# First pass of a two-layer attention kernel: half of the pair tiles after the image tiles, beside the statistics

## Chip, cores and metric

One core of a Trainium2 chip runs the kernel. The metric is the device time of one execution in microseconds, the median of three runs. TensorE (PE, with its weight load PEld), VectorE (DVE), ScalarE (ACT), GpSimd (POOL) and SyncE (SP, which here issues every DMA) each run their own instruction stream and wait on semaphores.

## What is computed

Two attention layers over x of shape (1, 128, 256, 256), each with a group norm before it and a residual after it. Cut to what matters here:

```python
# layer 0: h = group_norm(x); then
mu, var = mean and variance of h over all of (C, H, W)
x0   = (h - mu) * rsqrt(var + EPS) * ln_w + ln_b              # ln_w, ln_b: (128, 256, 256)
bias = einsum('hc,bcij->bhij', wb, x0)                        # 4 heads, from the image itself
...                                                           # q, k, v, g; softmax(q k + bias) v, gated, projected
x = x + layer0(h)
# layer 1: h = group_norm(x); then
bias = einsum('nijz,zh->nhij', pair_repr, bias_proj)[:, None] # 8 heads, from pair_repr (1, 256, 256, 128)
sim  = softmax(q k * scale) + bias                            # bias after the softmax
x = x + (sim v * gate) @ out_proj
```

The group norm's groups are the 8 last-axis columns, 32 groups; each needs the mean and variance over the whole image, so layer 0 can't begin before all of x has been read once.

## The kernel before

`prepare_weights` loads and splits the weights and starts the loads of the first two image tiles. `first_pass` then reads the image, the layer norm's weights and bias and the pair representation once, in 32 tiles of 8 rows. One image tile is three DMAs of 1 MB (x, ln_w, ln_b, line 209), one pair tile a DMA of 1 MB (line 243). All have two buffers. For each tile:

- DVE takes batch-norm statistics of the 32 groups (line 328), six numbers a group and tile, and POOL then multiplies x by ln_w in place (line 341).
- PE turns the pair tile by 16 transposes of 128x128 in four strips, one PSUM bank each (line 290). ACT copies strips 0 and 2 to SBUF (line 313), DVE strips 1 and 3 (line 303).
- PE projects ln_w, ln_b, the turned pair tile and x * ln_w onto the heads, eight matmul records each (line 277). ACT copies the four results to `fp_evac` (line 317), and SP stores them in eight small DMAs to the HBM scratch tensors `image_bias_parts` (line 256) and `pair_bias` (line 257).

SP's order for a tile: wait until the tile's buffers are free (all projections of it done, its pair tile turned), issue the four loads for the tile after next, then wait for the copy out and issue the eight stores.

When the pass's block is over, `finish_statistics` (first call) begins a new one. SP reads the three parts (six DMAs of 512 KB, line 378) and the pair bias (two of 1 MB, line 380) into SBUF. DVE aggregates 32 chunks of six numbers per group (line 386, 32 instructions of 192 elements); PE averages over the partitions with two small matmuls (lines 452, 454); DVE and ACT work out inverse roots of the group norm and of the layer norm; four DVE products over 128x2048 correct the layer 0 bias (lines 424 to 427). Then `layer0` runs 256 rows, storing its output and its statistics. `finish_statistics` (second call) aggregates those (33 chunks), turns layer 1's bias by 32 transposes beside it (lines 434 and 448), and `layer1` runs 128 rows of heads.

## Time and profile before

| | us |
|---|---|
| median of three runs | 4951.82 (4950.63 to 4952.84) |
| profiled execution | 4953.47 |
| its span | 4951.5 |
| PE busy | 4653.2 (94%) |
| DVE busy | 4023.9 (81%) |
| ACT busy | 3527.3 (71%) |
| POOL busy | 3466.7 (70%) |
| mean granted TensorE clock | 0.97 |

The span runs from the first instruction to the last, and the profiled execution has 2 us more around it. The page gives engine shares over the whole span, and PE's 94% is that of the two layers. The first pass and its statistics are the first 470 us, less than a tenth. There the other views are needed: windows give busy time, clock and DMA by stretch; the timeline gives each instruction's start and length, and in brackets how long its engine had been idle and what released it. A granted clock of 1.00 stands for 2.4 GHz and 0.50 for 1.2 GHz.

### The profile page before, as it was taken

What the parts mean: (1) busy time and instruction counts of PE and PEld (TensorE: products, weight loads), DVE (VectorE), ACT (ScalarE), POOL (GpSimd) and SP (SyncE); (2) the same over time, 40 slices, a digit from 0 to 9 for tenths busy, and PEclk for the clock granted to TensorE, in tenths of its full rate; (3) what the DMA queues carried; (4) which work ended last, traced back from release to release, by engine and by line L of the source; (5) the groups of instructions that cost most, each with busy time, mean ns of one, the idle gap of its engine ahead of it and who ended that gap; (6) DMA issues with size and microseconds to landing.
All of it is one profiled execution on the core that took longest, in us unless ns stands there. A gap on an engine that the chain in (4) does not pass through costs nothing. (4 is left out here: it accounts for less than half of the span.)

```text
span 4951.5 us, 149914 instructions
## 1 busy us (share of the span) xinstructions
PE 4653.2 (94%) x44087; PEld 3924.4 (79%) x44087; DVE 4023.9 (81%) x12779; ACT 3527.3 (71%) x11216; POOL 3466.7 (70%) x5926
## 2 busy tenths in 40 slices
PE   4663999999999999999999969999999999999999
PEld 2332888888888888888888858888888888888887
DVE  4445888888888888888888878888888888888887
ACT  2222888888888888888888846666666666666665
POOL 2332888888888888888888826666666666666665
PEclk8776999999999999999999979999999999999999
DMA  8995111111111111111111101111111111111111
GB/s 331 354 350 176 53 51 59 59 51 59 55 55 59 51 59 59 51 59 56 54 59 51 53 26 53 48 49 49 51 51 51 51 51 51 51 51 51 51 50 39
DMA packets 237329, 382.52 MB, mean 77 GB/s; under 512 B 18756, under 2 KB 156616, under 8 KB 224968
## 3 DMA queue, kind: packets, MB, share of 16 engines
q1 hardware_dynamic: 237256, 381.63, 23.0%
q8 instruction: 35, 0.57, 0.0%
q14 instruction: 38, 0.31, 0.0%
HBM read 309.21 MB, written 72.35 MB: 77 GB/s over the span
## 5 line engine op out<-in xcount | busy, mean ns | idle before, releaser
L1302 POOL TENSOR_SCALAR l_probs<-l_probs,l_inv 128x256 f32<-128x256 f32 x2048 | 944.3, 479 | 737.1 <-DVE l_inv L1207 731.7
L1126 ACT ACTIVATE l_probs<-bank,l_neg_max 128x256 f32<-128x256 f32 x2048 | 949.1, 482 | 486.2 <-DVE l_neg_max L1201 486.2
L545 POOL TENSOR_SCALAR l_probs<-l_probs,l_inv 128x256 f32<-128x256 f32 x2048 | 949.4, 479 | 269.0 <-DVE l_inv L796 269.0
L714 ACT ACTIVATE l_probs<-l_probs,l_neg_max 128x256 f32<-128x256 f32 x2048 | 1020.0, 518 | 1.5 <-DVE l_neg_max L788 1.3
L788 DVE CUSTOM_DVE_ANT_0 l_probs<-bank,bias 128x256 f32<-128x256 f32 x2048 | 779.8, 418 | 219.8 <-PE bank L655 215.6
L1201 DVE TENSOR_REDUCE l_neg_max<-bank 128x2 f32<-128x512 f32 x1024 | 646.7, 683 | 92.6 <-PE bank L1035 92.6
L1214 DVE TENSOR_TENSOR l_probs_t<-bank,bias 128x512 f32<-128x512 f32 x1024 | 674.1, 681 | 37.7 <-PE bank L1045 22.6
L655 PE MATMUL bank<-ident,l_probs 128*128 128x128 f32 x4096 | 629.4, 276 | 1.0 <-POOL l_probs L545 0.6
L1045 PE MATMUL bank<-ident,l_probs 128*128 128x128 f32 x4096 | 532.4, 273 | 3.1 <-DVE l_probs_t L1214 1.7
L668 PE MATMUL bank<-l_probs_t,l_v 128*64 128x256 f32 x4096 | 498.5, 385 | 0.7 <-DVE l_probs_t L810 0.5
L655 PEld LDWEIGHTS bank<-ident,l_probs 128*128 128x128 f32 x4096 | 463.9, 141 | 36.7 <-POOL l_probs L545 1.7
L1045 PEld LDWEIGHTS bank<-ident,l_probs 128*128 128x128 f32 x4096 | 460.6, 141 | 5.7 <-POOL l_probs L1302 3.3
L754 ACT ACTIVATE l_probs_t<-bank 128x512 f32<-128x512 f32 x512 | 309.2, 604 | 211.7 <-PE bank L655 211.7
L1126 ACT ACTIVATION_READ_ACCUMULATOR l_probs<-bank,l_neg_max 128x1 f32 x2048 | 434.8, 212 | 0.0
L714 ACT ACTIVATION_READ_ACCUMULATOR l_probs<-l_probs,l_neg_max 128x1 f32 x2048 | 429.6, 210 | 0.0
L810 DVE COPY l_probs_t<-bank 128x512 f32<-128x512 f32 x512 | 349.6, 683 | 53.6 <-PE bank L655 52.1
L668 PEld LDWEIGHTS bank<-l_probs_t,l_v 128*64 128x64 f32 x4096 | 271.7, 136 | 143.8 <-issue 1.1
L80 PE MATMUL bank<-l_xn_high,wqk_high 128*128 128x256 f32 x1024 | 331.2, 323 | 25.7 <-POOL l_xn_low L572 25.4
L642 PE MATMUL bank<-l_k_high,l_q_high 64*128 64x256 f32 x2048 | 342.0, 331 | 1.6 <-DVE l_k_low L804 1.6
L557 POOL TENSOR_TENSOR l_xf<-l_x,mean 128x256 f32<-128x256 f32 x256 | 301.5, 1178 | 58.7 <-DMA l_ln_b<-in_L_conv_ln_b_dram 58.7
L341 POOL TENSOR_TENSOR fp_x<-fp_x,fp_ln_w 128x2048 f32<-128x2048 f32 x32 | 145.6, 4549 | 268.4 <-DVE chunk_stats L328 268.4
L80 PE MATMUL bank<-l_xn_high,w_qk_high 128*128 128x256 f32 x1024 | 310.4, 303 | 3.5 <-POOL l_xn_low L1291 3.5
(193 smaller groups left out, 14002.8 us busy)
## 6 DMA issues: line engine op xcount, KB each, us to landing
fp_x<-in_x_dram SPq DMA_DIRECT2D x32, 1024.0 KB, 6.9
fp_ln_w<-in_L_conv_ln_w_dram SPq DMA_DIRECT2D x32, 1024.0 KB, 8.9
fp_ln_b<-in_L_conv_ln_b_dram SPq DMA_DIRECT2D x32, 1024.0 KB, 10.2
fp_pair<-in_L_conv_pair_repr_dram SPq DMA_DIRECT2D x32, 1024.0 KB, 12.1
l_x<-in_x_dram SPq DMA_DIRECT2D x128, 256.0 KB, 2.9
l_ln_w<-in_L_conv_ln_w_dram SPq DMA_DIRECT2D x128, 256.0 KB, 3.3
l_ln_b<-in_L_conv_ln_b_dram SPq DMA_DIRECT2D x128, 256.0 KB, 3.5
x<-l_y SPq DMA_DIRECT2D x128, 256.0 KB, 2.0
```

Source lines behind the costliest of these rows:

```text
L80: nc.tensor.matmul(out, lh, rh, start=start, stop=False)
L545: last = nc.gpsimd.tensor_scalar(probs[:, h, c], probs[:, h, c], inv[:, h, c:c + 1], 1.0, ALU.mult, ALU.mult)
L655: last = nc.tensor.transpose(b_t[h % 2][:, kc * W + qc * P:kc * W + (qc + 1) * P], probs[:, h, qc, kc * P:(kc + 1) * P], m.ident[:])
L668: last = nc.tensor.matmul(b_av[D0 * j:D0 * (j + 1), pair * W:(pair + 1) * W], v[:, k % 2, kc, h * D0:(h + 1) * D0], probs_t[:, k % 2, h, k ...
L714: last = nc.scalar.activation(probs[:, h, c], probs[:, h, c], ACT.Exp, bias=neg_max[:, h, c:c + 1], scale=-1.0, accum_out=total[:, h, c:c ...
L788: last = nc.vector.tensor_tensor_reduce(out=probs[:, h, c], in0=b_s[h % 2][:, c * W:(c + 1) * W], in1=m.bias0[:, c, h], scale=-1.0, scalar ...
L810: nc.vector.tensor_copy(probs_t[:, k % 2, h], b_t[h % 2][:].rearrange("p (a c) -> p a c", a=KC)).then_inc(t_ready[h], 1)
L1045: last = nc.tensor.transpose(b_t[TURNS.index(h) % 2][:, kc * W + qc * P:kc * W + (qc + 1) * P], probs[:, h, qc, kc * P:(kc + 1) * P], m.id ...
L1126: last = nc.scalar.activation(probs[:, h, c], b_s[h % 4][:, c * W:(c + 1) * W], ACT.Exp, bias=neg_max[:, h, c:c + 1], accum_out=total[:, h ...
L1201: nc.vector.tensor_reduce(neg_max[:, h], b_s[h % 4][:].rearrange("p (a c) -> p a c", a=KC), AX.X, ALU.max, negate=True).then_inc(max_ready, 1)
L1214: nc.vector.tensor_tensor(probs_t[:, k % 2, h], b_t[TURNS.index(h) % 2][:].rearrange("p (a c) -> p a c", a=KC), m.bias1[:, :, h], ALU.add) ...
L1302: last = nc.gpsimd.tensor_scalar(probs[:, h, c], probs[:, h, c], inv[:, h, c:c + 1], 1.0, ALU.mult, ALU.mult)
```

## The change

In `first_pass`, a pair tile now follows every second image tile, so that pair tiles 0 to 15 are handled beside the 32 image tiles. The pair work is split from the image work: turned strips are copied by ACT alone, the pair projection has its own copy out and its own four stores, the image parts have four stores of their own.

After the image tiles SP waits for the image stores, reads the parts back into SBUF within the same block, and then handles pair tiles 16 to 31 (`late_pairs`): for each, the load of the tile two further on, then the stores of this one. On PE the turns of the next tile stand ahead of the projection of this one, and on ACT likewise the copies. The two averaging matmuls stand in PE's order behind the projections of tiles 18 and 19, ACT's two roots behind tiles 20 and 22.

DVE aggregates the statistics of every four tiles in the pass into pieces (count 1, mean, variance), 32 instructions of 24 elements each; after the pass it aggregates eight pieces a group, and then does the same chain and the same four products as before. The chain's code is now in a class `Statistics` that both places use. The first call of `finish_statistics` is gone. The second one now loads layer 1's bias from HBM itself, before its transposes.

```diff
+class Statistics:
...
+    def vector(self, dve, pieces, with_layer_norm):
+        for g in range(NG):
+            last = nc.vector.bn_aggr(own[:, g, :], pieces(g))
+        last.then_inc(self.own_ready, 1)
+        chain = Chain(dve, self.step)
+        dve.wait_ge(self.own_ready, 1)
+        dve.wait_ge(self.mean_mm, 1)
...
+    def tensor(self, pe, n):
+        nc, m = self.nc, self.m
+        if n == 0:
+            pe.wait_ge(self.own_ready, 1)
+            nc.tensor.matmul(m.psum[0][:, 0:2 * NG], m.averager[:], self.own[:].rearrange("p g s -> p (g s)"), start=True, stop=True).then_inc(self.mean_mm, 1)
+        else:
+            pe.wait_ge(self.dev_ready, 1)
+            nc.tensor.matmul(m.psum[1][:, 0:NG], m.averager[:], self.dev[:], start=True, stop=True).then_inc(self.dev_mm, 1)
...
-    PAIRS = ROWS // 2
-    STORES = 2 * PAIRS
-    X_PART, W_PART, B_PART, PAIR_PART = range(4)
+    STRIPS = ROWS // 2
+    PERIOD = 4
+    X_PART, W_PART, B_PART = range(3)
+    b_part, b_pair, b_turned = m.psum[0:3], m.psum[3], m.psum[4:8]
...
+        def over_tiles(engine, image_tile, pair_tile):
+            def body(t):
+                for k in range(PERIOD):
+                    image_tile(PERIOD * t + k, 2 * t + k // 2, k % 2)
+                    if k % 2:
+                        pair_tile(2 * t + k // 2, t, k // 2)
+            loop_first_peeled(engine, TILES // PERIOD, body)
+        late_pairs = range(TILES // 2, TILES)
...
+            def store_pair(tile, i):
+                sp.wait_ge(pair_evacuated, tile + 1)
+                for c in range(STRIPS):
+                    rows = bass.ds(ROWS * tile + 2 * c, 2)
+                    sp.dma_start(pair_bias[:, rows, :].rearrange("h r k -> h (r k)"), pair_evac[i][32 * c:32 * c + NH1]).then_inc(pair_stored[i], 16)
             load_pair(0, 0)
             load_pair(1, 1)
             def body(t, first, last):
-                for i in range(2):
-                    if not last:
-                        load(2 * t + i + 2, i)
-                    store(2 * t + i, i)
-            loop_ends_peeled(sp, TILES // 2, body)
+                for k in range(PERIOD):
+                    if not (last and k >= PERIOD - 2):
+                        load_image(PERIOD * t + k + 2, k % 2)
+                    store_image(PERIOD * t + k, k % 2)
+                    if k % 2:
+                        load_pair(2 * t + k // 2 + 2, k // 2)
+                        store_pair(2 * t + k // 2, k // 2)
+            loop_ends_peeled(sp, TILES // PERIOD, body)
             for i in range(2):
-                sp.wait_ge(stored[i], 16 * STORES * TILES // 2)
+                sp.wait_ge(stored[i], 16 * STRIPS * TILES // 2)
+            for part, to in ((W_PART, bias_w), (X_PART, m.bias0), (B_PART, bias_b)):
+                for a in range(KC):
+                    sp.dma_start(to[:, a], image_parts[part, :, a * P:(a + 1) * P, :].rearrange("h p k -> p h k")).then_inc(parts_loaded, 16)
+            for tile in late_pairs:
+                if tile + 2 < TILES:
+                    load_pair(tile + 2, tile % 2)
+                store_pair(tile, tile % 2)
+            for i in range(2):
+                sp.wait_ge(pair_stored[i], 16 * STRIPS * TILES // 2)
...
+            def image_tile(tile, t, i):
+                pe.wait_ge(loaded[i], 48 * (t + 1))
+                project(b_part[W_PART], m.wb_t[:], wt[i]).then_inc(projected[W_PART], 1)
+                project(b_part[B_PART], m.wb_t[:], bt[i]).then_inc(projected[B_PART], 1)
+                pe.wait_ge(weighted, tile + 1)
+                project(b_part[X_PART], m.wb_t[:], xt[i]).then_inc(projected[X_PART], 1)
+            def pair_turns(tile, t, i):
+                pe.wait_ge(pair_loaded[i], 16 * (t + 1))
+                for j in range(STRIPS):
+                    wait(pe, copied, STRIPS * (tile - 1) + j + 1)
+                    for r in range(2):
+                        for e in range(2):
+                            last = nc.tensor.transpose(b_turned[j][:, (2 * r + e) * P:(2 * r + e + 1) * P], raw[i][:, 2 * j + r, e, :], m.ident[:])
+                    last.then_inc(transposed, 1)
+            def pair_project(tile, t, i):
+                pe.wait_ge(copied, STRIPS * (tile + 1))
+                wait(pe, pair_evacuated, tile)
+                project(b_pair, m.w_pair[:], turned[i]).then_inc(pair_projected, 1)
+            def pair_tile(tile, t, i):
+                pair_turns(tile, t, i)
+                pair_project(tile, t, i)
+            over_tiles(pe, image_tile, pair_tile)
+            pair_turns(late_pairs[0], late_pairs[0] // 2, 0)
+            for tile in late_pairs:
+                if tile + 1 < TILES:
+                    pair_turns(tile + 1, (tile + 1) // 2, (tile + 1) % 2)
+                pair_project(tile, tile // 2, tile % 2)
+                if tile == late_pairs[2]:
+                    pe.wait_ge(evacuated, TILES)
+                    statistics.tensor(pe, 0)
+                if tile == late_pairs[3]:
+                    statistics.tensor(pe, 1)
...
+            def image_tile(tile, t, i):
+                wait(act, stored[i], 16 * STRIPS * t)
+                for part in (W_PART, B_PART, X_PART):
+                    act.wait_ge(projected[part], tile + 1)
+                    last = nc.scalar.activation(evac[i][:, part], b_part[part][:], ACT.Copy)
+                last.then_inc(evacuated, 1)
+            def pair_copies(tile, t, i):
+                wait(act, pair_projected, tile - 1)
+                for j in range(STRIPS):
+                    act.wait_ge(transposed, STRIPS * tile + j + 1)
+                    nc.scalar.activation(turned[i][:, 2 * j:2 * j + 2, :].rearrange("p r (k e) -> p r e k", e=2),
+                                         b_turned[j][:].rearrange("p (r e k) -> p r e k", r=2, e=2), ACT.Copy).then_inc(copied, 1)
+            def pair_out(tile, t, i):
+                wait(act, pair_stored[i], 16 * STRIPS * t)
+                act.wait_ge(pair_projected, tile + 1)
+                nc.scalar.activation(pair_evac[i][:], b_pair[:], ACT.Copy).then_inc(pair_evacuated, 1)
+            def pair_tile(tile, t, i):
+                pair_copies(tile, t, i)
+                pair_out(tile, t, i)
+            over_tiles(act, image_tile, pair_tile)
+            pair_copies(late_pairs[0], late_pairs[0] // 2, 0)
+            for tile in late_pairs:
+                if tile + 1 < TILES:
+                    pair_copies(tile + 1, (tile + 1) // 2, (tile + 1) % 2)
+                pair_out(tile, tile // 2, tile % 2)
+                if tile == late_pairs[4]:
+                    statistics.scalar(act, 0)
+                if tile == late_pairs[6]:
+                    statistics.scalar(act, 1)
...
+            nc.vector.memset(pieces[:], 1.0).then_inc(counted, 1)
+            for t in range(TILES // PERIOD):
+                wait(dve, piece_ready, t)
+                for k in range(PERIOD):
+                    dve.wait_ge(loaded[k % 2], 48 * (2 * t + k // 2 + 1))
                     for g in range(NG):
-                        last = nc.vector.bn_stats(stats[:, g, tile, :], xt[i][:, :, g * GROUP:(g + 1) * GROUP])
+                        last = nc.vector.bn_stats(stats[:, g, k, :], xt[k % 2][:, :, g * GROUP:(g + 1) * GROUP])
                     last.then_inc(measured, 1)
-                    wait(dve, projected[PAIR_PART], tile - 1)
-                    for j in range(1, PAIRS, 2):
-                        dve.wait_ge(transposed, PAIRS * tile + j + 1)
-                        copy_turned(nc.vector.tensor_copy, i, j).then_inc(copied_dve, 1)
-            loop_first_peeled(dve, TILES // 2, body)
+                dve.wait_ge(measured, PERIOD * (t + 1))
+                dve.wait_ge(counted, 1)
+                for g in range(NG):
+                    last = nc.vector.bn_aggr(pieces[:, g, t, 1:3], stats[:, g, 0:PERIOD, :])
+                last.then_inc(piece_ready, 1)
+            dve.wait_ge(piece_ready, TILES // PERIOD)
+            dve.wait_ge(evacuated, TILES)
+            chain = statistics.vector(dve, lambda g: pieces[:, g], True)
...
-                for part, to in ((1, w_part), (0, m.bias0), (2, b_part)):
-                    for a in range(KC):
-                        sp.dma_start(to[:, a], biases[0][part, :, a * P:(a + 1) * P, :].rearrange("h p k -> p h k")).then_inc(loaded, 16)
-                for a in range(KC):
-                    sp.dma_start(m.bias1[:, a], biases[1][:, a * P:(a + 1) * P, :].rearrange("h p k -> p h k")).then_inc(pair_loaded, 16)
-                sp.wait_ge(pair_loaded, 16 * KC)
+            for a in range(KC):
+                sp.dma_start(m.bias1[:, a], pair_bias[:, a * P:(a + 1) * P, :].rearrange("h p k -> p h k")).then_inc(pair_loaded, 16)
...
+            pe.wait_ge(pair_loaded, 16 * KC)
+            for h in range(NH1):
...
-        finish_statistics(nc, m, "gs0", stats, lambda g: W // 8, True, (image_parts, pair_bias))
         layer0(nc, m, x, ln_w, ln_b, x1, stats)
-        finish_statistics(nc, m, "gs1", stats, lambda g: W // 8 + (g < NG - 4), False, turn_bias=True)
+        finish_statistics(nc, m, stats, lambda g: W // 8 + (g < NG - 4), pair_bias)
         layer1(nc, m, x1, out)
```

## Rows read from the trace of the kernel before

**Rows 1.** windows of the trace: engines' busy time (instructions), clock, DMA share, GB/s

```profile
50.00:100.00 50.00, 30.67 (x194) 17.24 (x195) 22.76 (x141) 14.65 (x24) 18.21 (x4) 0.77 0.95 352
...
200.00:250.00 50.00, 31.12 (x196) 16.73 (x195) 22.56 (x137) 14.65 (x24) 18.55 (x5) 0.77 0.98 358
...
430.00:440.00 10.00, 0.00 (x0) 0.00 (x0) 10.00 (x12) 0.00 (x0) 0.00 (x0) 0.50 1.09 347
```

**Rows 2.** the timeline of the first tiles: start, length, engine, line, operation [idle before]

```profile
24.53 1.01 SPq L243 DMA_DIRECT2D fp_pair<-in_L_conv_pair_repr_dram  x2
...
28.78 4.52 POOL L341 TENSOR_TENSOR fp_x<-fp_x,fp_ln_w 128x2048 f32<-128x2048 f32 x1 [27.29 <-DVE chunk_stats L328]
...
30.06 3.68 PE L290 MATMUL bank<-ident,fp_pair 128*128 128x128 f32 x16 [15.78 <-DMA fp_pair<-in_L_conv_pair_repr_dram]
...
37.24 1.97 PE L290 MATMUL bank<-ident,fp_pair 128*128 128x128 f32 x16
...
37.38 0.34 SPq L209 DMA_DIRECT2D fp_x<-in_x_dram  x1
...
43.78 0.31 SPq L257 DMA_DIRECT2D pair_bias<-fp_evac  x1
...
45.83 0.30 SPq L257 DMA_DIRECT2D pair_bias<-fp_evac  x1
...
47.33 4.15 DVE L328 BATCH_NORM_STATS2 chunk_stats<-fp_x 128x64 f32 x32 [7.39 <-DMA fp_ln_b<-in_L_conv_ln_b_dram]
```

**Rows 3.** the timeline of the last tile, the statistics and layer 0's first load

```profile
406.52 4.25 DVE L328 BATCH_NORM_STATS2 chunk_stats<-fp_x 128x64 f32 x32 [4.44 <-DMA fp_ln_b<-in_L_conv_ln_b_dram]
...
409.43 3.49 PE L290 MATMUL bank<-ident,fp_pair 128*128 128x128 f32 x16 [4.00 <-DMA fp_pair<-in_L_conv_pair_repr_dram]
...
410.57 0.64 ACT L313 ACTIVATE fp_pair_t<-bank 128x512 f32<-128x512 f32 x1 [4.47 <-PE bank L290]
...
415.46 1.07 PE L277 MATMUL bank<-fp_x,wb_t 128*32 128x512 f32 x8
...
416.60 0.60 ACT L317 ACTIVATE fp_evac<-bank 128x512 f32<-128x512 f32 x1 [0.31 <-PE bank L277]
...
420.43 0.30 SPq L257 DMA_DIRECT2D pair_bias<-fp_evac  x1
...
423.32 0.97 SPq L378 DMA_DIRECT2D gs_w_part<-image_bias_parts  x2
...
423.35 28.31 DVE L386 BATCH_NORM_AGGREGATE gs_own<-chunk_stats 128x2 f32<-128x192 f32 x32 [9.71 <-PEq L224]
...
468.90 0.34 SPq L511 DMA_DIRECT2D l_x<-in_x_dram  x1
```

**Rows 4.** clock after pauses of PE: the timeline at three places, a window

```profile
135.60 3.21 PE L290 MATMUL bank<-ident,fp_pair 128*128 128x128 f32 x16 [3.57 <-DMA fp_pair<-in_L_conv_pair_repr_dram]
...
2879.48 0.39 PE L80 MATMUL bank<-l_o_high,wrep_t_high 128*128 128x256 f32 x1 [2.17 <-DVE l_o_low L823]
...
208.00:209.00 1.00, 0.00 (x0) 0.00 (x0) 1.00 (x10) 0.00 (x0) 0.00 (x0) 0.50 1.24 308
```

**Rows 5.** the timeline of the hand-over to layer 1

```profile
2884.52 29.07 DVE L386 BATCH_NORM_AGGREGATE gs_own<-chunk_stats 128x2 f32<-128x198 f32 x32 [0.30 <-PEq L466]
...
2884.53 5.01 PE L448 MATMUL bank<-ident,bias 128*128 128x128 f32 x32 [4.07 <-PEq L466]
```

**Rows 6.** the timeline of layer 0, POOL beside DVE

```profile
601.75 0.73 POOL L561 TENSOR_TENSOR l_xf<-l_xf,rstd 128x256 f32<-128x256 f32 x1
...
602.10 0.61 DVE L847 BATCH_NORM_STATS2 chunk_stats<-l_y 128x64 f32 x4
...
606.65 0.86 DVE L823 TENSOR_TENSOR l_o_low<-l_o,l_o_high 128x512 fp32r<-128x512 f32 x1
...
606.92 1.19 POOL L557 TENSOR_TENSOR l_xf<-l_x,mean 128x256 f32<-128x256 f32 x1
```

More of the change, by code:

```diff
@@ new lines, in first_pass @@
+        projected = [sem(f"projected_{part}") for part in ("x", "w", "b")]
+        statistics = Statistics(nc, ctx, m, "gs0")
+        block = ctx.enter_context(nc.Block())
+        def over_tiles(engine, image_tile, pair_tile):
[5 more added lines that the diff above has]
+            loop_first_peeled(engine, TILES // PERIOD, body)
@@ new lines, in first_pass, with _, load_pair, load_image @@
+        late_pairs = range(TILES // 2, TILES)
+        @block.sync
+        def _(sp):
+            def load_pair(tile, i):
+                wait(sp, transposed, STRIPS * (tile - 1))
+                sp.dma_start(raw[i][:], pair[bass.ds(ROWS * tile, ROWS)].rearrange("q (p e) z -> p q e z", e=2)).then_inc(pair_loaded[i], 16)
+            def store_pair(tile, i):
[3 more added lines that the diff above has]
+                    sp.dma_start(pair_bias[:, rows, :].rearrange("h r k -> h (r k)"), pair_evac[i][32 * c:32 * c + NH1]).then_inc(pair_stored[i], 16)
+            def load_image(tile, i):
+                for part in (X_PART, W_PART, B_PART):
+                    wait(sp, projected[part], tile - 1)
+                image.load(sp, tile, i)
+            def store_image(tile, i):
+                sp.wait_ge(evacuated, tile + 1)
+                for c in range(STRIPS):
+                    rows, mine = bass.ds(ROWS * tile + 2 * c, 2), evac[i][32 * c:32 * c + NH0]
+                    sp.dma_start(image_parts[:, :, rows, :].rearrange("s h r k -> h s (r k)"), mine).then_inc(stored[i], 16)
+            load_pair(0, 0)
+            load_pair(1, 1)
+            def body(t, first, last):
+                for k in range(PERIOD):
[15 more added lines that the diff above has]
+                store_pair(tile, tile % 2)
+            for i in range(2):
+                sp.wait_ge(pair_stored[i], 16 * STRIPS * TILES // 2)
@@ new lines, in _, with project @@
+        @block.tensor
+        def _(pe):
+            def project(bank, weights, rows):
+                for c in range(STRIPS):
+                    last = nc.tensor.matmul(bank[32 * c:32 * c + 32, :], weights, rows[:, 2 * c:2 * c + 2, :].rearrange("p r k -> p (r k)"),
+                                            start=True, stop=True, tile_position=(0, 32 * c))
+                return last
+            def image_tile(tile, t, i):
+                pe.wait_ge(loaded[i], 48 * (t + 1))
+                wait(pe, evacuated, tile)
+                project(b_part[W_PART], m.wb_t[:], wt[i]).then_inc(projected[W_PART], 1)
[28 more added lines that the diff above has]
+                    statistics.tensor(pe, 1)
@@ L271, in _ @@
+        @block.vector
+        def _(dve):
+            statistics.vector(dve, lambda g: stats[:, g, 0:chunks(g), :], False)
+        @block.scalar
+        def _(act):
+            for h in range(NH1):
+                act.wait_ge(bias_mm, h + 1)
+                nc.scalar.activation(m.bias1[:, :, h], b_bias[h % 6][:].rearrange("p (a c) -> p a c", a=KC), ACT.Copy).then_inc(bias_out, 1)
+            statistics.scalar(act, 0)
         @block.tensor
         def _(pe):
-            def project(part, tile, weights, rows):
-                wait(pe, evacuated, tile)
-                for c in range(PAIRS):
-                    last = nc.tensor.matmul(m.psum[part][32 * c:32 * c + 32, :], weights, rows[:, 2 * c:2 * c + 2, :].rearrange("p r k -> p (r k)"),
-                                            start=True, stop=True, tile_position=(0, 32 * c))
-                last.then_inc(projected[part], 1)
@@ L457, in layer0 @@
+            pe.wait_ge(pair_loaded, 16 * KC)
+            for h in range(NH1):
+                wait(pe, bias_out, h - 5)
+                for kc in range(KC):
+                    for qc in range(KC):
+                        last = nc.tensor.transpose(b_bias[h % 6][:, kc * W + qc * P:kc * W + (qc + 1) * P], m.bias1[:, qc, h, kc * P:(kc + 1) * P], m.ident[:])
+                last.then_inc(bias_mm, 1)
+            statistics.tensor(pe, 0)
+            statistics.tensor(pe, 1)
 def layer0(nc, m, x, ln_w, ln_b, x1, stats):
```

243 lines of the change are left out of this document (79 added, 164 removed).

## Prediction

> **What bounds the kernel now.** I read the page first (busy shares, the 40 slices), then stretches of 50 and 10 us over the first 480 us, where the whole change lies, then the timeline of the first tiles, of the last tile and of the statistics, and last the hand-over to layer 1. From 50 to 400 us the 16 DMA engines are 95 to 98% busy at 352 to 358 GB/s while no compute engine passes 65% [rows 1]: the first pass is bound by transfers. From the third image tile (statistics begin at 47.33) to the last (406.52) there are 29 steps, so 12.39 us a tile [rows 2, 3]. Of these the pair megabyte takes 2.9 us (from the image landing at 406.52 to the turns at 409.43); the rest, 9.5 us, is three image megabytes and eight small stores. At 2.85 us a megabyte the stores get the remaining (12.39 - 11.4)/8 = 0.12 us each. Then comes a stretch where DMA is nearly idle: the last X projection ends at 416.5 (415.46 + 1.07), the parts are read back from 423.32, the 32 aggregations take 28.3 us from 423.35, the scalar chain and four 2.3 us products follow, and layer 0 issues its first load at 468.90 [rows 3]. These 52.4 us are what the change wants to cover. After 469 nothing is changed until the hand-over at 2884.
>
> **Part 1: the pass moves less.** Sixteen of 32 pair megabytes leave it. Two image tiles now carry six image megabytes, one pair megabyte and 12 stores: 7 x 2.85 + 12 x 0.12 = 21.4 us, against 24.8. Does latency bound it instead? A tile's buffers are free after its X projection, 415.46 + 1.07 - 406.52 = 10.0 us after landing [rows 3], some 0.6 more where the matmuls find the low clock, which is usual here as PE now pauses 5 us between W/B and X. Three megabytes issued into an empty queue at 37.38 were there at 47.33: 9.95 us [rows 2]. Together 20.6 us for two tiles: just under 21.4, so transfers still bind, but with under 1 us of slack, and the queue will sometimes run dry. First projection: POOL ends at 33.3, X slow, 35.1; tile 2 lands at 45.0; tile 30 at 45.0 + 14 x 21.4 = 344.6; tile 31 9.0 later; its X projection ends at 364.2. If each of 14.5 rounds lost 0.5 us it would be 371.5. I take 366.7, a third of that, because SP has finished its stores long before the next buffer is free. Gain at this point: 416.5 - 366.7 = 49.8 us.
>
> All turned copies go to ACT (four of 0.64 us a pair tile [rows 3]); it stays under half busy. DVE loses its two copies of 0.69 us and gets 32 aggregations of 24 elements after every fourth tile. One of 192 elements takes 28.31/32 = 0.885 us, 28 of 198 and four of 192 take 29.07 us [rows 3, 5]: 4.5 ns an element, which leaves 0.13 us for 24 elements, 4.2 us a group. DVE is idle from 4.3 us after landing to the next landing over 9 us after; cost nothing, covered by the transfer. Bounds: 0.11 (proportional) to 0.885 us (all fixed); see the rivals. The final aggregation over 8 pieces shrinks from 28.3 to 4.2 us as well.
>
> **Part 2: the tail.** Times from the last X projection, P. SP waits for pair tile 15 before it reads the parts back: turns 3.7, last copy 0.75, projection 1.05, copy out 0.7, four stores at 0.34 apart ((45.83 - 43.78)/6 [rows 2]): P + 7.7. Before, the same wait ended at 423.32, P + 6.8. The 3 MB of parts take some 11 us more (before, 5 MB were through by 440 [rows 1]), and pair 18, issued behind them on SP's queue, lands at P + 22. Tiles 16 and 17 were turned by P + 13; PE then idles. The mean matmul stands behind tile 18, at P + 28, the second behind 19, the roots behind ACT's tiles 20 and 22; the four products end near P + 65. So the statistics are covered by the late tiles, wherever they stand.
>
> The late tiles then set the end, and they are no stream. SP's order is load(T+2), store(T), load(T+3): a load waits until four stores are issued, these for the copy out of T, that for the projection of T, which on PE stands behind the turns of T+1. With two buffers the round of two tiles is: load, turns, projection, copy out, four stores. A load of 1 MB into an empty queue: issued 24.53, its turns start at 30.06, 5.5 us with a second one behind it [rows 2]; 9.95 us for three, less 2 x 2.85, gives 4.3. I take 5.0. Turns: 3.5 to 3.7 us at 1.2 GHz (409.43), 1.97 at 2.4 GHz (37.24) [rows 2, 3]. Projection 1.05, handing over 0.1, copy out 0.60, stores 1.36, handing over 0.1 [rows 3]. At the low clock 5.0 + 3.65 + 1.05 + 0.8 + 1.36 = 11.9; at the full one ACT's four copies end last (0.6 + 4 x 0.65 = 3.2 after the turns begin), 5.0 + 3.2 + 0.75 + 1.36 = 10.3. A stream would need 2 x 2.85 + 8 x 0.12 = 6.7 for the same two tiles.
> Pair 20 lands at P + 33.7. Full clock: turns of 30 begin at 33.7 + 5 x 10.3 = 85, those of 31 4.6 later, then two projections, copy out, four stores and 2.5 us to their landing and the new block (as 420.7 to 423.3): P + 98.6. Low clock: the start comes 1.5 us later, six rounds cost 1.6 more each: P + 111.
> Which clock? A pause of 2.17 us left PE fast (2879.48, 0.39 us a matmul), one of 3.57 left most of the turns slow (135.60), and in one of 4.5 us (205.3 to 209.8) the granted clock stood at 0.50 by 208 [rows 4]. The full-clock round leaves pauses of about 1.6 and 2.6 us, the low one 1.2 us twice: mostly fast, with relapses. I take P + 101.5.
>
> **A rule of the skill.** The rows above put the part of a small load that isn't transfer at 1.5 to 2.6 us, and a round pays it in full. The Trainium skill, "DMA: Bandwidth & Descriptors", section "Anatomy of one DMA", has a fixed cost of about 2.0 us per DMA plus bytes over 436 GB/s. By it a load would take 4.4 us and the round 0.6 us less, P + 95; it speaks against the change, since that cost is covered only by loads issued early.
>
> **Part 3: layer 1's bias.** Its two 1 MB loads move from the covered stretch to the hand-over: 8 to 11 us before the turns, which last 5 us there, 7 if slow. Beside them DVE aggregates for 29.07 us [rows 5], so at most 21 of 29 us are used: nothing, and 20 us if that cover were gone. One block less saves 0.5 us, within the rounding.
>
> **Sum.** First load of layer 0: 366.7 + 101.5 = 468.2, against 468.9: -0.7 us. The rest of the span (4951.5 of 4953.5 us in the profiled run) is as before. The profiled run is 1.7 us above the median of three, 4951.8; forecast 4951.1. About 50 us are won in the pass and 49 given back by late tiles that go one load at a time. Unknowns: pass -2.5 to +5, tail -3 to +9.5; own range 4945 to 4962.
>
> **Rivals.** Changes under 0.2% (9.9 us) can hardly be told from none.
> A. Slower: the low clock in the late tiles. Condition: PE's pause in a round reaches some 3 us, or the load takes 5.5 us. Each round costs 11.9 instead of 10.3, and if the queue also runs dry in the pass: 371.5 + 111 - 468.9 = +13.6, 4965. For it: pauses of 3.57 us and more made the turns slow in nearly every tile. Against: the round's pauses are shorter.
> B. Slower: the aggregations in the pass. If an aggregation of 24 elements costs 0.3 us, DVE is late for the next tile and I get +11; at 0.885, +140. A variant is that they hold up POOL's multiplication beside them, which frees X. In layer 0 a DVE operation with two SBUF inputs (606.65) goes with a POOL operation of 1.19 us instead of 0.73, while statistics beside POOL (602.10) leave it at 0.73 [rows 6]. If the aggregations held POOL for 4 us in every fourth tile it were 8 x 3.5 = 28 us, 4980.
> The Trainium skill, "SBUF — State Buffer", section "SBUF: two separate sides", has DVE and GpSimd exclude each other only for a two-port mode or two SBUF inputs of DVE; an aggregation has one, so by it this variant falls away.
> C. Faster: image loads alone run quicker than the mixed queue. 9.95 us for three megabytes, with 2.1 of it fixed (the middle of 1.5 to 2.6), is 2.6 a megabyte; then 6 x 2.6 + 2.85 + 1.44 = 19.9, the latency bound of 20.6 takes over, 14.5 x 0.8 = 12 us less: 4939, with the tail at full clock 4935. Against: in the steady pass no stretch went beyond 358 GB/s.
> D. The overlap fails, the statistics come after the late tiles. The program order excludes it; it would take the root behind tile 22 to be later than P + 90.
>
> **Chances.** Forecast, within 0.2%: 0.50. A (over 9.9 us slower): 0.20. B: 0.09. C: 0.20. D: 0.01. So faster 0.20, same 0.50, slower 0.30. The range takes in C's 4937 and A's 4967; outside it stay most of B and the ends of C, under 2 in 10.
>
> **What would show it.** Statistics of image tiles 21.4 us apart for two; last X projection at 365 to 370; DVE's groups of aggregations at 4 to 5 us, POOL still 4.55; late turns in pairs, 10 to 12 us a round, DMA under 250 GB/s there; layer 0's first load at 463 to 475; hand-over unchanged at 29 us of aggregation. The forecast is wrong if the late rounds come near 7 us or over 13, if the pass steps are under 20.6, or if an aggregation of 24 elements takes over 0.25 us.

## The result and the profile after

The changed kernel takes 4961.43 us (median of 20 runs, 4955.84 to 4967.29) against 4951.68 us for the kernel before (20 runs, 4944.49 to 4953.17). The ratio is 1.0022, 95% interval 1.0015 to 1.0028: slower by 9.75 us, where 0.7 us less was forecast. The profiled execution has a span of 4961.3 us, 9.8 more than before. Of all executions reported here one was in a slower state of the chip, 9730.74 us at a granted clock of 0.67, among the eleven of the change without the partial aggregation, and no ratio counts it.

First the stretches, as in [rows 1]. Columns: engines' busy time with the number of instructions, granted clock, DMA share, GB/s.

```profile
200.00:250.00 50.00, 28.15 (x160) 10.09 (x152) 20.63 (x161) 14.51 (x24) 22.41 (x5) 0.74 0.94 354
...
350.00:400.00 50.00, 27.26 (x174) 14.69 (x172) 16.35 (x126) 19.33 (x33) 9.02 (x2) 0.79 0.67 219
...
410.00:420.00 10.00, 5.35 (x33) 3.93 (x35) 1.99 (x9) 5.64 (x10) 0.00 (x0) 0.75 0.73 223
...
450.00:460.00 10.00, 5.96 (x28) 3.98 (x29) 0.00 (x0) 2.82 (x5) 0.00 (x0) 0.66 0.64 211
```

Up to 350 us the picture is the one of before: DMA engines near 0.95, 350 GB/s. Then the late part begins, and there no resource is full: DMA falls to 0.64 to 0.73 in the stretches shown (before, the stretch at 430 was the read-back at 1.09 and the one after it was empty), PE is busy for a little over half of these 10 us stretches and has a clock of 0.75 and 0.66. So the question is which wait follows which.

The pass itself, from the timeline (start, length, engine, line, operation, idle time before it):

```profile
227.69 4.15 DVE L468 BATCH_NORM_STATS2 chunk_stats<-fp_x 128x6 f32<-128x64 f32 x32 [4.74 <-DMA fp_ln_b<-in_L_conv_ln_b_dram]
...
231.87 4.04 DVE L473 BATCH_NORM_AGGREGATE fp_pieces<-chunk_stats 128x2 f32<-128x24 f32 x32
...
231.91 4.52 POOL L490 TENSOR_TENSOR fp_x<-fp_x,fp_ln_w 128x2048 f32<-128x2048 f32 x1 [4.37 <-DVE chunk_stats L468]
...
240.24 4.14 DVE L468 BATCH_NORM_STATS2 chunk_stats<-fp_x 128x6 f32<-128x64 f32 x32 [4.32 <-DMA fp_ln_b<-in_L_conv_ln_b_dram]
...
249.99 4.14 DVE L468 BATCH_NORM_STATS2 chunk_stats<-fp_x 128x6 f32<-128x64 f32 x32 [5.61 <-DMA fp_ln_b<-in_L_conv_ln_b_dram]
```

A round of two tiles takes 21.67 us: the statistics of tile 2 start at 45.87 and those of tile 30 at 349.23, 14 rounds later (303.36/14). The group of 32 aggregations at 231.87 takes 4.04 us and is over long before DVE's next tile; POOL's multiplication beside it (231.91) takes 4.52 us, as in other tiles.

Then the tail, which answers to [rows 3]:

```profile
357.68 4.14 DVE L468 BATCH_NORM_STATS2 chunk_stats<-fp_x 128x6 f32<-128x64 f32 x32 [4.30 <-DMA fp_ln_b<-in_L_conv_ln_b_dram]
...
361.85 4.04 DVE L473 BATCH_NORM_AGGREGATE fp_pieces<-chunk_stats 128x2 f32<-128x24 f32 x32
...
366.47 1.18 PE L381 MATMUL bank<-fp_x,wb_t 128*32 128x512 f32 x8 [2.27 <-POOL fp_x L490]
...
368.40 4.21 DVE L236 BATCH_NORM_AGGREGATE gs_own<-fp_pieces 128x2 f32<-128x24 f32 x32 [2.50 <-ACT fp_evac L429]
...
390.71 3.67 PE L399 MATMUL bank<-ident,fp_pair 128*128 128x128 f32 x16 [11.19 <-DMA fp_pair<-in_L_conv_pair_repr_dram]
...
398.32 0.43 PE L282 MATMUL bank<-gs_own,averager 128*128 128x64 f32 x2
...
402.90 3.67 PE L399 MATMUL bank<-ident,fp_pair 128*128 128x128 f32 x16 [4.15 <-DMA fp_pair<-in_L_conv_pair_repr_dram]
...
406.51 1.91 PE L381 MATMUL bank<-fp_pair_t,w_pair 128*32 128x512 f32 x8
...
408.55 0.60 ACT L442 ACTIVATE fp_pair_evac<-bank 128x512 f32<-128x512 f32 x1 [1.30 <-PE bank L381]
...
408.59 1.95 PE L399 MATMUL bank<-ident,fp_pair 128*128 128x128 f32 x16
...
409.17 1.29 SPq L339 DMA_DIRECT2D pair_bias<-fp_pair_evac  x4
...
410.51 0.40 SPq L333 DMA_DIRECT2D fp_pair<-in_L_conv_pair_repr_dram  x1
...
416.18 3.68 PE L399 MATMUL bank<-ident,fp_pair 128*128 128x128 f32 x16 [4.65 <-DMA fp_pair<-in_L_conv_pair_repr_dram]
...
434.33 2.29 DVE L484 TENSOR_TENSOR bias<-bias,fp_bias_b 128x2048 f32<-128x2048 f32 x1
...
467.50 3.67 PE L399 MATMUL bank<-ident,fp_pair 128*128 128x128 f32 x16 [5.03 <-DMA fp_pair<-in_L_conv_pair_repr_dram]
...
481.58 0.38 SPq L588 DMA_DIRECT2D l_x<-in_x_dram  x1
```

The last X projection ends at 366.47 + 1.18 = 367.65 (called P below), 48.9 us earlier than before. Tile 18's turns begin at 390.71, tile 20's at 402.90, tile 22's at 416.18, tile 30's at 467.50: (467.50 - 402.90)/5 = 12.9 us a round of two tiles. One round can be followed in the lines: turns of tile 20 (402.90), projection of tile 19 behind them (406.51), its copy out (408.55), its four stores (409.17), only then the load of tile 22 (410.51), and its turns at 416.18.

The granted clock in that round, during the turns of tile 20, the projection of tile 19 and the turns of tile 21:

```profile
403.00:406.50 3.50, 3.50 (x16) 3.17 (x16) 0.00 (x0) 1.90 (x3) 0.00 (x0) 0.50 0.68 232
...
406.60:408.40 1.80, 1.80 (x9) 0.17 (x9) 0.00 (x0) 0.63 (x1) 0.00 (x0) 0.54 0.00 0
...
408.70:410.40 1.70, 1.70 (x17) 1.59 (x15) 0.57 (x3) 1.53 (x4) 0.00 (x0) 1.00 0.10 17
```

The mean matmul is done at 398, the last of the four products at 436.6, 45 us before layer 0 may begin: the statistics are covered, and the late tiles alone set the end. Layer 0's first load is issued at 481.58; before it was 468.90.

The hand-over to layer 1 answers to [rows 5]:

```profile
2896.74 1.02 SPq L508 DMA_DIRECT2D bias<-pair_bias  x2
...
2896.77 29.07 DVE L236 BATCH_NORM_AGGREGATE gs_own<-chunk_stats 128x2 f32<-128x198 f32 x32 [0.30 <-PEq L543]
...
2906.17 0.60 ACT L518 ACTIVATE bias<-bank 128x512 f32<-128x512 f32 x1 [15.21 <-PE bank L528]
...
2912.00 1.28 ACT L275 ACT_TABLE_LOAD   x1
```

The bias loads are now issued at its start; ACT's first copy out of a turned head starts 9.4 us after that instead of 1.1, and the last ends before 2912, 14 us before DVE's aggregation is through at 2925.8. Hidden, as forecast. The hand-over starts 12.25 us later than before, and layer 1's first load (2931.24 against 2918.99) too. The profiled span is only 9.8 us longer, as layer 1 itself took 2.4 us less in this execution; with single executions of this kernel 11 us apart, that is not a finding.

### The profile page after: what moved, and what is told of

It reads as the page before. It is cut to its first block and busy times, and to the rows that moved or that the text cites. A ratio compares the mean times of both kernels' runs of the same rounds, so it can differ in the third digit from the quotient of the medians.

```text
span 4961.3 us, 148921 instructions
## 1 busy us (share of the span) xinstructions
PE 4681.7 (94%) x44087; PEld 3908.6 (79%) x44087; DVE 3988.8 (80%) x12972; ACT 3557.4 (72%) x11280; POOL 3464.6 (70%) x5926
## 5 line engine op out<-in xcount | busy, mean ns | idle before, releaser
L719 PEld LDWEIGHTS bank<-l_k_high,l_q_high 64*128 64x128 f32 x2048 | 191.3, 183 | 142.4 <-issue 142.1
```

Of the source, the lines that this page charges most:

```text
L719: last = nc.tensor.matmul(b_s[j][:, c * W:(c + 1) * W], q[a][channels, k % 2, pair, c * P:(c + 1) * P], kk_[b][channels, k % 2, pair], sta ...
```

## Experiments

Four questions: is the tail a serial round, and what is in it; does the clock matter; is the partial aggregation of use; and does a stream of late tiles get below the kernel before? Each kernel was timed against the kernel before on its chip.

**The pause filled with matmuls.**

```diff
                 if tile == late_pairs[3]:
                     statistics.tensor(pe, 1)
+                if tile % 2 == 0 and tile >= late_pairs[2]:
+                    for _ in range(4):
+                        project(b_part[B_PART], m.wb_t[:], wt[0])
```

> The changed kernel, with sixteen unused matmuls (four projections into a spare bank, some 3.4 us) behind each even late pair tile from tile 18 on, in the pause in which PE waits for the next load. Theory 1 (the late tiles are a serial round of two tiles: load 5.6, turns, projection, copy out, four stores issued; and PE's pause of 4.5 us puts each round's first turns and projection at the low clock): with the pause filled the turns of the even tile take 2.0 us and the projection 1.1 instead of 3.65 and 1.9, the round falls from 12.9 to about 10.9 us, layer 0's first load from 481.6 to about 470, the kernel is 12 us faster than the changed one, near 4950. Rival theory 2 (the round is set by the DMAs, and PE's speed only fills its waiting): round stays at 12.9 us, time at 4961. Rival 3 (the filling matmuls delay the turns more than the clock gives): round over 13 us, slower than 4961.

Measured: 4954.01 us, ratio 1.0006 (0.9996 to 1.0016). The timeline shows the turns of tiles 20, 21, 22, 24 and 26:

```profile
403.91 1.97 PE L399 MATMUL bank<-ident,fp_pair 128*128 128x128 f32 x16 [0.69 <-DMA fp_pair<-in_L_conv_pair_repr_dram]
...
407.14 1.97 PE L399 MATMUL bank<-ident,fp_pair 128*128 128x128 f32 x16
...
415.31 1.97 PE L399 MATMUL bank<-ident,fp_pair 128*128 128x128 f32 x16 [1.77 <-DMA fp_pair<-in_L_conv_pair_repr_dram]
...
426.86 1.97 PE L399 MATMUL bank<-ident,fp_pair 128*128 128x128 f32 x16 [1.91 <-DMA fp_pair<-in_L_conv_pair_repr_dram]
...
437.36 1.97 PE L399 MATMUL bank<-ident,fp_pair 128*128 128x128 f32 x16 [0.90 <-DMA fp_pair<-in_L_conv_pair_repr_dram]
```

All are at the full clock (1.97 us), tile 20's included, and the granted clock from 403.90 to 463.00 is 1.00. PE still waits 0.7 to 1.9 us for each even tile's load, so the added matmuls don't hold the turns up. A round takes (437.36 - 403.91)/3 = 11.15 us. The first load of layer 0 comes at 472.64, 8.9 us earlier. So the low clock accounts for 1.8 us of a round and some 9 us of the tail. The rival, that PE's speed only fills waiting, is out; so is the third theory. The gain is smaller than expected: 7.4 us between the medians instead of 12, 11.15 us a round instead of 10.9, layer 0's first load at 472.64 instead of 470.

**Loads ahead of stores.**

```diff
             for tile in late_pairs:
                 if tile + 2 < TILES:
                     load_pair(tile + 2, tile % 2)
-                store_pair(tile, tile % 2)
+                if tile > late_pairs[0]:
+                    store_pair(tile - 1, (tile - 1) % 2)
+            store_pair(TILES - 1, 1)
```

> The changed kernel with one line of SP's order turned in the late part: the load of tile T+2 now stands ahead of the stores of tile T-1 instead of T, so that a load waits only for its buffer to be turned. Theory 1 (serial round with the stores in it): the round becomes load 5.6 + turns 2.0 to 3.7 + some 1 us, 8.5 to 10 us instead of 12.9; over six rounds 17 to 26 us less, layer 0's first load at 456 to 464, the kernel 4936 to 4944, faster than the kernel before. Rival theory 2 (the load itself, or the rate of small packets, bounds it): round stays above 12 us and the time at 4961.

Measured: 4932.00 us, ratio 0.9963 (0.9948 to 0.9977). Turns of tiles 20, 21 and 31, the load of tile 22, layer 0's first load:

```profile
399.18 1.97 PE L401 MATMUL bank<-ident,fp_pair 128*128 128x128 f32 x16 [0.95 <-DMA fp_pair<-in_L_conv_pair_repr_dram]
...
401.17 0.40 SPq L333 DMA_DIRECT2D fp_pair<-in_L_conv_pair_repr_dram  x1
...
403.10 1.97 PE L401 MATMUL bank<-ident,fp_pair 128*128 128x128 f32 x16 [0.62 <-DMA fp_pair<-in_L_conv_pair_repr_dram]
...
442.97 1.97 PE L401 MATMUL bank<-ident,fp_pair 128*128 128x128 f32 x16 [1.51 <-DMA fp_pair<-in_L_conv_pair_repr_dram]
...
451.54 0.38 SPq L590 DMA_DIRECT2D l_x<-in_x_dram  x1
```

The load of tile 22 is issued at 401.17, the moment tile 20 has been turned. A tile takes (442.97 - 399.18)/11 = 3.98 us, a round 8.0, and PE now pauses for 1.5 us at most. From tile 20 on all turns are at the full clock without any help:

```profile
399.20:442.00 42.80, 32.89 (x266) 21.04 (x266) 13.26 (x24) 32.17 (x58) 0.00 (x0) 1.00 0.91 283
```

One line of order is worth 30 us (481.58 to 451.54), more than the 17 to 26 us expected. The serial round stood in SP's order, through the stores. It had brought the low clock with it: of the 4.9 us that a round loses here, the first experiment gives 1.8 to the clock alone, and by that estimate 3.1 are the wait for the stores.

**Half of each late load.**

```diff
-                    load_pair(tile + 2, tile % 2)
+                    load_pair(tile + 2, tile % 2, ROWS // 2)
```

> The changed kernel, with the loads of the late pair tiles 18 to 31 cut to four of their eight rows; the other rows keep what the buffer held, so layer 1's bias is wrong for half of those rows. All turns, copies and stores stay. Theory 1 (a serial round with the whole load in it): the load loses half of its transfer, 1.4 us, and keeps a fixed part of some 2.7; round 12.9 -> 11.5 us, 8 us less in all, 4953. Should the shorter pause also lift the clock, the round is near 10 and the kernel at 4944. Rival (the load is mostly fixed cost): under 0.5 us a round, 4959.

Measured: 4950.45 us, ratio 0.9999 (0.9990 to 1.0009). The load of tile 22, its turns and those of tile 24:

```profile
404.14 0.40 SPq L333 DMA_DIRECT2D fp_pair<-in_L_conv_pair_repr_dram  x1
...
408.08 2.54 PE L399 MATMUL bank<-ident,fp_pair 128*128 128x128 f32 x16 [2.68 <-DMA fp_pair<-in_L_conv_pair_repr_dram]
...
418.47 2.68 PE L399 MATMUL bank<-ident,fp_pair 128*128 128x128 f32 x16 [2.96 <-DMA fp_pair<-in_L_conv_pair_repr_dram]
```

From issue to turns 3.94 us (404.14 to 408.08). The even tiles 20 to 30 take 3.80 to 4.07 us, 3.93 in the mean, and in the changed kernel 5.31 to 5.84, 5.55 in the mean: half a megabyte costs some 1.6 us, and a straight line through the two sizes leaves 2.3 us. This is an estimate, as a second load follows some 3 us behind each of these. The round shown is 418.47 - 408.08 = 10.4 us, and over five rounds (the turns of tile 20 start at 397.75, those of tile 30 at 450.25) it is 10.5, 2.4 less than in the changed kernel. What exceeds the 1.6 us goes with the quicker turns: PE's pause before tile 22 has shrunk from 4.7 to 2.7 us, and the turns take 2.5 instead of 3.7, while the projection behind them still takes 1.9. Both parts of the expectation are seen in the rounds; the kernel's time lies between its 4953 and its 4944. (The pass of this execution was 2.7 us quicker than that of the changed kernel, so rounds are compared.)

**The partial aggregation alone,** in the kernel before:

```diff
-                        last = nc.vector.bn_stats(stats[:, g, tile, :], xt[i][:, :, g * GROUP:(g + 1) * GROUP])
+                    last = nc.vector.bn_stats(stats[:, g, tile % 4, :], xt[i][:, :, g * GROUP:(g + 1) * GROUP])
...
+                if tile % 4 == 3:
+                    for g in range(NG):
+                        last = nc.vector.bn_aggr(pieces[:, g, tile // 4, 1:3], stats[:, g, 0:4, :])
```

> The kernel before, with the partial aggregation alone: DVE aggregates every fourth tile in the pass, and 8 pieces after it. All pair tiles stay in the pass. Theory 1: in the pass nothing changes (12.4 us a tile, DVE idle anyway), the last aggregation falls from 28.3 to 4.2 us, so layer 0's first load comes 24 us earlier at 445, the kernel is at 4928. Rival: the aggregations in the pass delay the turned copies on DVE behind them (4.2 us in every fourth tile), the tile's buffers come free later and the pass gets 8 x 2 to 4 us longer: 4944 to 4960.

Measured: 4928.15 us, ratio 0.9953 (0.9937 to 0.9970), and in a second set 4926.10 us, ratio 0.9954 (0.9937 to 0.9970). The last group in the pass, the final one, the first product, layer 0's first load:

```profile
413.43 4.03 DVE L341 BATCH_NORM_AGGREGATE pieces<-chunk_stats 128x2 f32<-128x24 f32 x32
...
423.73 4.04 DVE L395 BATCH_NORM_AGGREGATE gs_own<-pieces 128x2 f32<-128x24 f32 x32 [6.27 <-PEq L224]
...
436.04 2.29 DVE L433 TENSOR_TENSOR gs_w_part<-gs_w_part,mean 128x2048 f32<-128x2048 f32 x1 [0.67 <-DMA gs_b_part<-image_bias_parts]
...
445.80 0.34 SPq L520 DMA_DIRECT2D l_x<-in_x_dram  x1
```

The pass is unchanged (the last tile's statistics start at 406.16, before at 406.52), the final aggregation takes 4.04 us instead of 28.31, and layer 0 begins at 445.80, 23.1 us earlier. The first product now waits 0.67 us for the parts: with the aggregation gone, the read-back is as late as the chain. The time is the 4928 us expected, and the rival, a longer pass, is out. The same thing was expected of the second set, where layer 0's first load comes at 444.09:

> The kernel before with the partial aggregation alone, once more, to stand beside the two others on one chip: 4928 +- 2, layer 0's first load at 445.8.

**The change without the partial aggregation.**

```diff
-            chain = statistics.vector(dve, lambda g: pieces[:, g], True)
+            chain = statistics.vector(dve, lambda g: stats[:, g, 0:TILES, :], True)
```

> The changed kernel without the partial aggregation: DVE aggregates all 32 chunks after the image tiles, 28.3 us, beside the late pair tiles. Theory 1 (the statistics are covered by the late tiles): the mean matmul waits for it about as long as it does now for its place behind tile 18 (P + 30), at most 1 us more; layer 0's first load at 481 to 483, the kernel at 4961 +- 2. Rival (the aggregation still is on the path): 24 us slower, 4985.

> The changed kernel without the partial aggregation once more, for its trace: the mean matmul at 399 to 401 (398.3 with the pieces), layer 0's first load within 2 us of 481.6.

Measured: 4961.89 us, ratio 1.0022 (1.0012 to 1.0032), and 4962.62 us in the one execution of the second set, whose timeline has the aggregation, the mean matmul and tile 20's turns:

```profile
366.75 28.31 DVE L236 BATCH_NORM_AGGREGATE gs_own<-chunk_stats 128x2 f32<-128x192 f32 x32 [6.76 <-ACT fp_evac L429]
...
396.47 0.43 PE L282 MATMUL bank<-gs_own,averager 128*128 128x64 f32 x2
...
400.97 3.68 PE L399 MATMUL bank<-ident,fp_pair 128*128 128x128 f32 x16 [4.06 <-DMA fp_pair<-in_L_conv_pair_repr_dram]
```

28.31 us of aggregation cost nothing here: the mean matmul follows at 396.47, its place in PE's order, and layer 0's first load comes at 480.22 (481.58 with the pieces). From the last X projection on both tails last 114 us (366.00 to 480.22, 367.65 to 481.58). The change's two halves cover the same 24 us. Either one hides the aggregation; together the second finds nothing left.

**A stream of late tiles.** Tiles 18 to 31 go to eight load buffers: the two of before and the six image buffers, which are free by then.

```diff
+        def late_buffer(tile):
+            j = (tile - late_pairs[0]) % 8
+            return raw[j][:] if j < 2 else (xt, wt, bt)[(j - 2) % 3][(j - 2) // 3][:].rearrange("p r (e z) -> p r e z", e=2)
...
+            for tile in late_pairs[2:8]:
+                load_late(tile)
             for tile in late_pairs:
-                if tile + 2 < TILES:
-                    load_pair(tile + 2, tile % 2)
+                if tile + 8 < TILES:
+                    sp.wait_ge(transposed, STRIPS * (tile + 1))
+                    load_late(tile + 8)
                 store_pair(tile, tile % 2)
```

> The changed kernel, with the late pair tiles loaded into eight buffers: the two of before and the six image buffers, which nobody needs after the last image tile. SP issues tiles 18 to 23 at once behind the parts, the others when a buffer has been turned. Theory 1: with loads issued early the late tiles are a stream bound by ACT (four copies of 0.65 us and a copy out of 0.6, 3.2 to 3.4 us a tile) at full PE clock; pair 18 still starts 23 us after the last X projection, 14 tiles of 3.3 us and 5 us of end: first load of layer 0 at 438 to 444, the kernel 4918 to 4924. Rival (something else than the serial load paces the tiles, such as the stores or the DMA rate with 1 KB packets): over 4.5 us a tile, 4935 or more.

Measured: 4936.14 us, ratio 0.9969 (0.9959 to 0.9979), no better than two buffers in the right order, where 4918 to 4924 was expected. Layer 0's first load comes at 451.93. Of the waits between 378 and 450 us (total, times, longest) this one explains it:

```profile
ACT fp_pair_evac L462 <- DMA pair_bias<-fp_pair_evac: 11.6, 4, 10.1
```

The longest of them ends at 409.25: ACT's copy out of tile 18 waits 10.1 us until the stores of tile 16, which has the same output buffer, have landed. That tile had been copied out by 380.68, but SP issued its stores only at 400.32, behind the loads of tiles 18 to 24, seven megabytes; issuing each of the last five of these loads took SP 2.8 to 3.4 us. (The expectation of a later experiment counts six.)

**Parts behind the loads.** Here SP issues the six read-backs after the loads of tiles 18 to 25 instead of before them.

> As with eight buffers, and the parts are read back behind the loads of tiles 18 to 25 instead of ahead of them. Theory: PE's pause of 11 us in which it waits for tile 18 behind the 3 MB of parts goes; tiles 18 to 25 run at 3.3 us, tile 26 then waits some 4 us behind the parts: layer 0's first load 4 to 8 us earlier than with eight buffers alone, 432 to 438, kernel 4912 to 4918. Rival: the parts come too late for the four products (they begin some 60 us after the last X projection now, and could begin at 36), which then set the end: no gain.

Measured: 4937.08 us, ratio 0.9971 (0.9962 to 0.9981); first load of layer 0 at 452.73. The expected gain isn't there, and not for the rival's reason: the mean matmul (384.65 against 399.09) and the turns of tiles 18 to 20 came 12 to 14 us earlier, and then the same copy out, that of tile 18, waited 24.7 us instead of 10.1, for stores that now had the parts ahead of them as well. It ended at 409.40, against 409.25, and the turns of tile 21 start at 412.46, against 412.30: all that was won at the start is lost in this wait.

**Four output buffers,** added to either order:

```diff
+        def late_out(tile):
+            i = tile % 2
+            late = tile // 2 - TILES // 4
+            if tile % 4 < 2:
+                return pair_evac[i][:], pair_stored[i], 16 * STRIPS * (TILES // 4 + late // 2)
+            return evac[i][:, 0], stored[i], 16 * STRIPS * (TILES // 2 + late // 2)
```

> As with eight buffers (parts read back first), and the copies out of the late tiles go to four buffers instead of two (the two of before and the parts' buffers), each with its own count of stores. With eight load buffers ACT's copy out waited 10.1 us at one place for stores that were queued behind six megabytes of loads. Theory: that wait is what kept eight buffers from being a stream; with four outputs most of it goes, layer 0's first load at 441 to 447 instead of 451.9, the kernel at 4921 to 4928. Rival: the stores still take as long to come through, a tile's outputs come free one by one, and the time stays within 2 us of 4936.

> Eight load buffers, four output buffers, and the parts read back behind the loads of tiles 18 to 25. If the transfers bound the tail (14 MB of pairs, 3 MB of parts, stores: about 52 us from 8 us after the last X projection on) and ACT keeps 3.3 us a tile, layer 0's first load comes at 431 to 438, the kernel at 4912 to 4920. Rival: the queue holds loads ahead of stores all the time and four outputs don't do: as parts_behind, 4937.

Measured: 4926.69 us (0.9952, 0.9935 to 0.9968) with the parts first, 4927.24 us (0.9957, 0.9941 to 0.9974) with the parts behind, and 4926.10 us for the pieces alone in the same set. Stretches of the first, as in the first table of this section:

```profile
375.00:400.00 25.00, 12.00 (x88) 8.83 (x80) 0.35 (x3) 9.63 (x17) 0.00 (x0) 0.80 1.03 328
...
400.00:425.00 25.00, 21.07 (x163) 13.75 (x161) 8.12 (x25) 19.46 (x37) 0.00 (x0) 0.93 1.09 355
...
425.00:444.00 19.00, 18.11 (x151) 11.13 (x149) 5.75 (x3) 16.60 (x31) 0.00 (x0) 1.00 0.49 150
```

With the parts first, the DMA engines are full up to 425 us, at 328 to 355 GB/s. The last six tiles then follow each other at 2.89 us with PE busy for 18.11 of 19.00 us and DMA at 0.49, and layer 0 begins at 447.68. This is what was expected (4921 to 4928; the first load 0.7 us later than its 441 to 447), and the copy out's longest wait is 4.1 us: the wait for the output buffer was what held eight load buffers back. With the parts behind, one such wait is much longer, between 372 and 445 us:

```profile
ACT fp_pair_evac L481 <- DMA pair_bias<-fp_pair_evac: 17.7, 1, 17.7
```

So the expected 4912 to 4920 was missed: the pause at the start was gone, but tile 20's copy out now waited 17.7 us in the middle, and layer 0 begins at 445.32. What the runs show is that the moved megabytes are not saved: with the parts first, a tail in which they stream is bound by transfers until 425 us, as the pass was, and by PE after that. It ends close to where the pieces alone end (445.80 and 444.09), and no run here shows more than coincidence in that. The ratios of the three, 0.9952, 0.9957 and 0.9954, can't be told apart, and nothing here beats the kernel before with pieces alone. Whether fewer late tiles would, say eight, wasn't tried.

## Why the prediction was wrong

The time, 4961.43 us, is just inside the range of 4945 to 4962, but the forecast was a kernel 0.7 us faster and it is 9.75 us slower. The sentence on chances says that the range takes in 4937 and 4967; it takes in neither. The parts against the trace of the changed kernel:

- **The pass** was right: 21.67 us a round against 21.4, last X projection at 367.65 against 366.7, DVE's aggregation of 24 elements 4.04/32 = 0.126 us against 0.13. Rival C (image loads faster alone) didn't happen. Rival B fell: POOL's 4.52 us beside the aggregations is its usual time (4.49 to 4.52). What the Trainium skill, "SBUF — State Buffer", section "SBUF: two separate sides", says of a DVE operation with one SBUF input agrees with this trace.
- **The hand-over** was right: 29.07 us of aggregation, the loads hidden, 14 us of cover left.
- **The tail up to tile 20** was nearly right: tile 18 at P + 23.1 against 22, tile 20 at P + 35.3 against 33.7.
- **The late rounds** are the step that failed. The mechanism was right, and the second experiment shows it, but the term of the sum was mis-sized: a round was taken at the full clock, 10.3 us, and measured 12.9. The full-clock tail was 33.7 to tile 20, five rounds of 10.3 and 13.4 of end, 98.6; the trace has 35.3, five rounds of 12.9 and 14.1 of end, 113.9 (481.58 - 367.65). Of the 15.3 us between them 13.1 are the rounds. The prediction allowed 2.9 us for relapses of the clock, so 101.5, and was 12.4 short.
- **Rival A,** with its condition (a pause of some 3 us or a load of 5.5), is what happened, and it was priced short as well: 11.9 us a round. Its end, P + 111, is also wrongly added up: 98.6 + 1.5 + 6 x 1.6 is 109.7. That its total of 4965 is near the measured 4961 is in part luck: its tail is too short and its pass, 371.5, too long.
- **Inside the round** two terms were too small for either clock. The load was to take 5.0 us, and those of the even tiles 20 to 30 took 5.3 to 5.8 (410.51 to 416.18 for tile 22). The turns took 3.67, as in the low-clock bound, but the projection behind them 1.9 (406.51), where I had 1.05. Added to the low-clock round of 11.9 us, 0.6 and 0.85 make 13.35, against 12.9 measured (in two of the five rounds the clock rose earlier); the larger part of the miss, 1.6 of 2.6 us, is that I chose the full clock.
- **Why the clock was low.** I expected two pauses of 1.6 and 2.6 us in a round. The loads of two tiles are issued 3 us apart (410.51, 413.61), so the second one is there when the first has been handled: PE does both at once and then waits once, 4.2 to 5.0 us. Its first turns of each round then run at the low level, in most rounds the projection behind them too (granted 0.50 and 0.54 above), and the rest at the full one. In the round of tile 24 the projection already takes 1.07 us, in that of tile 26 1.59. The first experiment, which does nothing but fill the pause, takes 1.8 us from the round.
- **What I didn't see** was how much of the round was merely order. I named the stores between the loads, priced a stream at 6.7 us and passed on. The experiment that moves them gives 8.0 us a round.
- **The forecast's frame**, 50 us won and 49 given back, hid that the two halves of the change aim at the same time. Of the 52 us of statistics 24 can be had without any late tile, and then 16 late tiles, 46 us of transfer at 2.85 us each, stand against the 29 us that are left between the last X projection and layer 0 (416.91 to 445.80 with the pieces alone).

The page I cited, the Trainium skill's "DMA: Bandwidth & Descriptors", section "Anatomy of one DMA — SWDGE (gpsimd) path", gives 2.0 us plus bytes over 436 GB/s, which as an estimate makes 4.4 us for a late load. That fit is for DMAs issued from GpSimd, which the prediction doesn't say, and all of these are issued by SP. The trace has 5.3 to 5.8 us; whole and half load together put the fixed part at 2.3 us, near the page's, and the rate at some 320 GB/s, below it. The measurement decides. In the changed kernel each round pays this fixed part in full.

## What to carry to other kernels

When work is moved out of a transfer-bound stretch to cover a chain, write down its own round in the new place, buffer by buffer and in the order of the issuing queue: a load behind a store inherits the store's whole wait. Ask also whether the chain can be made shorter where it is; here some 23 us came off by using an idle engine, and the larger rearrangement added nothing to that. And where a round has pauses like the 4 to 5 us here, price it at the low TensorE clock for what follows the pause, the operation behind the first one too.

## What the runs showed of the hardware

- A pause of 4.2 to 5.0 us in each round put PE's next work at the low clock, in most rounds for 5.5 us (turns 3.67, projection 1.9 us against 1.97 and 1.06), while rounds with pauses of up to 1.5 us, and up to 1.9 us where filled, stayed at the full clock throughout. A pause of 2.7 us lies between: the granted clock was still 1.00 in the first microsecond after it (408 to 409 us with half loads) and 0.50 from 410.6 to 412.4; the turns took 2.5 us, the projection 1.9.
- Small stores behind large loads on one queue wait for them: behind seven loads of 1 MB a copy out waited 10.1 us, behind eight and the parts' 3 MB 17.7 us with four output buffers and 24.7 us with two. With several loads outstanding SP's issue of the next took 2.8 to 3.4 us instead of 0.4 (eight buffers, from 385 us on), so what stood behind them in the program was issued late.
- An aggregation of batch-norm statistics costs 0.126 us with 24 elements and 0.885 with 192, about 4.5 ns an element.
